# The mixer's output projection taken from rounded halves of z and of its weights, in three passes

## What is computed

```python
proj = jnp.einsum('bld,pd->blp', hidden_states, W_in)
gate = proj[..., :INTER]
...                                   # conv, chunked scan -> y  (B, L, INTER)
g = y * jax.nn.silu(gate)
gg = g.reshape(B, L, G, INTER // G)
var = jnp.mean(gg * gg, axis=-1, keepdims=True)
gg = gg * lax.rsqrt(var + EPS)
out_norm = gg.reshape(B, L, INTER) * norm_weight
return jnp.einsum('bli,di->bld', out_norm, W_out)
```

## Time and profile before

| what | before |
|---|---|
| median of 3 runs | 2531.27 us (2529.53 to 2531.35) |
| the profiled execution | 2531.68 us, span of the trace 2530.0 us |
| PE busy over the span | 2259.8 us, 89% |
| DVE, ACT, POOL busy | 1836.3 us (73%), 1435.5 us (57%), 1289.7 us (51%) |
| mixer's part (about 265 to 1518 us) | PE busy 1211.3 of 1253.0 us, granted clock 1.00 |
| output projection L981 | 256.4 us of PE, 1024 entries |

### The profile page before, as it was taken

The page is one execution under the profiler, slowest core; times in us unless marked ns, Lnnn a source line. Parts: engine busy times, 40 slices in busy tenths (PEclk is TensorE's granted clock), DMA queues, the critical chain, the costliest instruction groups (busy, mean ns, idle before and its releaser), DMA issues. The chain is left out here.

```text
span 2530.0 us, 45593 instructions
## 1 busy us (share of the span) xinstructions
PE 2259.8 (89%) x16164; PEld 1793.2 (71%) x16164; DVE 1836.3 (73%) x3256; ACT 1435.5 (57%) x2461; POOL 1289.7 (51%) x1275
## 2 busy tenths in 40 slices
PE   4996999999999999999999972799999995799992
PEld 2785788888888888888888862688888884444432
DVE  5875777777777777777777746677777776777755
ACT  1333778877878787877878851122222224266661
POOL 3451676777767777676876770354554540000000
PEclk9997999999999999999999995899999998799996
DMA  2002112112121121211211220100000002122214
GB/s 90 1 22 111 44 53 74 53 45 90 45 80 47 45 91 45 82 45 53 82 53 57 75 67 1 36 28 21 28 21 28 27 8 96 59 76 81 76 60 137
DMA packets 93441, 141.19 MB, mean 56 GB/s; under 512 B 23713, under 2 KB 62977, under 8 KB 91969
## 3 DMA queue, kind: packets, MB, share of 16 engines
q1 hardware_dynamic: 91200, 133.96, 16.1%
q10 hardware_dynamic: 2048, 4.72, 0.6%
HBM read 118.12 MB, written 20.32 MB: 55 GB/s over the span
## 5 line engine op out<-in xcount | busy, mean ns | idle before, releaser
L1081 DVE SCALAR_TENSOR_TENSOR mix_cv<-mix_pp,mix_cw,mix_cv 128x384 f32<-128x384 f32 (+4 forms) x864 | 490.8, 571 | 215.0 <-ACT mix_cv L999 194.2
L1220 POOL TENSOR_TENSOR ffn_hl<-ffn_h,ffn_hh 128x512 fp32r<-128x512 f32 x112 | 144.9, 1293 | 250.8 <-ACT ffn_hh L1278 250.8
L1024 ACT ACTIVATE mix_lm<-mix_pd 128x512 f32<-128x512 f32 x256 | 153.3, 599 | 205.1 <-PE mix_pd L915 203.1
L851 POOL TENSOR_TENSOR mix_ce<-mix_ce,mix_cv 128x1024 f32<-128x1024 f32 x112 | 266.8, 2382 | 0.0
L75 PE MATMUL mix_pp<-l0in_XH,mix_w_lo 128*128 128x384 f32 (+2 forms) x576 | 243.6, 423 | 22.9 <-DVE mix_w_lo L1069 16.2
L981 PE MATMUL mix_px<-mix_wo,mix_z 128*128 128x256 f32 x1024 | 256.4, 394 | 0.0
L1707 DVE TENSOR_REDUCE att_tops<-att_psc 128x1 f32<-128x512 f32 (+3 forms) x384 | 189.9, 550 | 55.5 <-PE att_psc L1655 32.2
L857 POOL TENSOR_TENSOR mix_zt<-mix_zsq 128x256 f32<-128x256 f32 x128 | 94.2, 736 | 243.0 <-ACT mix_zsq L1032 243.0
L1731 ACT ACTIVATE att_pr<-att_pst 128x1024 f32<-128x1024 f32 (+7 forms) x256 | 156.5, 657 | 103.5 <-PE att_pst L1672 73.5
L1278 ACT ACTIVATE ffn_hh<-ffn_h 128x512 fp32r<-128x512 f32 x112 | 71.1, 635 | 249.0 <-DVE ffn_h L1301 249.0
L981 PEld LDWEIGHTS mix_px<-mix_wo,mix_z 128*128 128x128 f32 x1024 | 186.8, 192 | 20.6
(11 more groups left out here) (332 smaller groups left out, 6873.2 us busy)
## 6 DMA issues: line engine op xcount, KB each, us to landing
mix_ce<-ecs SPq DMA_DIRECT2D x112, 512.0 KB, 3.7
mix_w_raw<-in_w_in SPq DMA_DIRECT2D x8, 1280.0 KB, 5.6
a_part<-att_sums SPq DMA_DIRECT2D x32, 256.0 KB, 5.1
ffn_raw<-in_wgu SPq DMA_DIRECT2D x56, 128.0 KB, 2.2
mix_ll<-cs SPq DMA_DIRECT2D x384, 4.0 KB
mix_wo<-in_w_out SPq DMA_DIRECT2D x8, 512.0 KB, 6.6
ffn_draw<-in_wd SPq DMA_DIRECT2D x28, 128.0 KB, 2.1
q<-qkv_part SPq DMA_DIRECT2D x24, 128.0 KB, 1.9
```

The source lines that it names most:

```text
L851: pool.tensor_tensor(ce[o][:, :, :], ce[o][:, :, :], cv[:, CT_C, cols_of(c)].unsqueeze(1).to_broadcast([P, GH, Q]), ALU.mult).then_inc(ce_ ...
L1024: act.activation(lm[o][:, 4 * i:4 * i + 4, :].rearrange("p h l -> p (h l)"), pd[:, :], ACT.Exp).then_inc(l_done, 1)
L1081: last = dve.scalar_tensor_tensor(out, of, cw[:, g, ct, 3 - d:4 - d], out, ALU.mult, ALU.add)
```

## The change

Rounded halves: `hi` is a value rounded to TensorE's fp32r format, `lo` the remainder in the same format. The product z times wo becomes zh·wo_l + zh·wo_h + zl·wo_h. The output weights are split once a group (`wo_h` by ScalarE, `wo_l` by GpSimd, in the slot `c % 16 == 1`), and z in every slot (`zh` by ScalarE behind the gate's SiLU, `zl` by GpSimd between `zs` and `xdt`). z and `wo` have one buffer now. The table constants that were loaded through the second z buffer go through `xtok0`.

```diff
-        wo = s.sb("wo", [P, 2, GX // P, D])
+        wo = s.sb("wo", [P, GX // P, D])
+        wo_h, wo_l = (s.sb(n, [P, GX // P, D], F32R) for n in ("wo_h", "wo_l"))
-        z = [s.sb(f"z{j}", [P, NX, Q]) for j in range(2)]
+        z = s.sb("z", [P, NX, Q])
+        zh, zl = (s.sb(n, [P, NX, Q], F32R) for n in ("zh", "zl"))
...
                     if c % 16 == 2 and g < G0 - 1:
                         wait(sp, proj_done, 36 * g)
                         wait(sp, gate_done, 16 * g)
-                        wait(sp, op_done, 16 * g)
+                        sp.wait_ge(wo_split, g + 1)
...
-                        pool.tensor_tensor(wo[:, o, :, :], wo[:, o, :, :],
+                        pool.tensor_tensor(wo[:, :, :], wo[:, :, :],
-                                           ALU.mult).then_inc(wo_split, 1)
+                                           ALU.mult).then_inc(wo_scaled, 1)
...
                         pool.tensor_tensor(zs[:, :], zt[:, 0, :], zt[:, 1, :], ALU.add).then_inc(zs_done, 1)
+                        if p % 16 == 0:
+                            pool.wait_ge(wo_cut, p // 16 + 1)
+                            pool.tensor_tensor(wo_l[:, :, :], wo[:, :, :], wo_h[:, :, :].bitcast(F32), ALU.subtract).then_inc(wo_split, 1)
+                        pool.wait_ge(zh_done, p + 1)
+                        wait(pool, op_done, p)
+                        pool.tensor_tensor(zl[:, :, :], z[:, :, :], zh[:, :, :].bitcast(F32), ALU.subtract).then_inc(zl_done, 1)
...
+                        pe.wait_ge(zh_done, p + 1)
                         for k in range(NX):
-                            last = pe.matmul(px[:, 0:D], z[p % 2][:, k, :], wo[:, p // 16 % 2, k, :],
-                                             start=k == 0, stop=k == NX - 1)
+                            pe.matmul(px[:, 0:D], zh[:, k, :], wo_l[:, k, :], start=k == 0, stop=False)
+                            pe.matmul(px[:, 0:D], zh[:, k, :], wo_h[:, k, :], start=False, stop=False)
+                        pe.wait_ge(zl_done, p + 1)
+                        for k in range(NX):
+                            last = pe.matmul(px[:, 0:D], zl[:, k, :], wo_h[:, k, :], start=False, stop=k == NX - 1)
                         last.then_inc(op_done, 1)
...
+                    if 0 <= p < NC:
+                        wait(act, op_done, p)
+                        if p % 16 == 0:
+                            act.wait_ge(wo_scaled, p // 16 + 1)
+                            act.activation(wo_h[:, :, :], wo[:, :, :], ACT.Copy).then_inc(wo_cut, 1)
+                        act.activation(flat(zh), flat(z), ACT.Copy).then_inc(zh_done, 1)
...
-                        wait(dve, op_done, p - 1)
-                        wait(dve, sq_done, p - 1)
-                        dve.tensor_tensor(z[p % 2][:, :, :], py[:, :].rearrange("p (k l) -> p k l", k=NX),
+                        wait(dve, sq_done, p)
+                        wait(dve, zh_done, p)
+                        wait(dve, zl_done, p)
+                        dve.tensor_tensor(z[:, :, :], py[:, :].rearrange("p (k l) -> p k l", k=NX),
```

More of the change, by code:

```diff
@@ L694, in mixer @@
         tabs_in, norm_in, const, made, self_v, zeroed = (s.sem(n) for n in ("tabs_in", "norm_in", "const", "made", "self_v", "zeroed"))
-        w_in_s, wx_split, wg_split, wo_split, hi_made, hi_first = (
-            s.sem(n) for n in ("w_in", "wx_split", "wg_split", "wo_split", "hi_made", "hi_first"))
+        w_in_s, wx_split, wg_split, wo_scaled, wo_cut, wo_split, hi_made, hi_first, zh_done, zl_done = (
+            s.sem(n) for n in ("w_in", "wx_split", "wg_split", "wo_scaled", "wo_cut", "wo_split", "hi_made", "hi_first", "zh_done",
+                               "zl_done"))
         cs_in, ecs_in = ([s.sem(f"{n}{j}") for j in range(2)] for n in ("cs_in", "ecs_in"))
@@ L707, in mixer @@
             s.sem(n) for n in ("xdt_done", "xdtd_done", "ce_done", "cd_done", "zt_done", "zs_done", "rs_done"))
-        rows_f, ones_f = z, zsq
+        ones_f = zsq
         def flat(ap):
@@ L770, in load_weights @@
                     sp.dma_start(w_raw[:, :, :], w_in[g]).then_inc(w_in_s, 16)
-                    sp.dma_start(wo[:, g % 2, :, :], w_out[g]).then_inc(w_in_s, 16)
+                    sp.dma_start(wo[:, :, :], w_out[g]).then_inc(w_in_s, 16)
                 def load_row(i):
@@ L783, in _ @@
                 for i in range(2):
-                    sp.dma_start(flat(rows_f[i])[0:KD_ROWS, :], sel_rows[:, i * 512:(i + 1) * 512]).then_inc(const, 16)
+                    sp.dma_start((flat(z) if i == 0 else xtok[0])[0:KD_ROWS, :], sel_rows[:, i * 512:(i + 1) * 512]).then_inc(const, 16)
                 sp.dma_start(flat(ones_f)[0:KD_ROWS, 0:2 * Q], one_rows).then_inc(const, 16)
@@ L1013, in _ @@
                         act.activation(rl[o][:, 4 * i:4 * i + 4, :].rearrange("p h l -> p (h l)"),
-                                       flat(rows_f[i])[0:KD_ROWS, :], ACT.Copy).then_inc(made, 1)
+                                       (flat(z) if i == 0 else xtok[0])[0:KD_ROWS, :], ACT.Copy).then_inc(made, 1)
                 act.wait_ge(tabs_in, 48)
@@ L1031, in _ @@
                         wait(act, zt_done, p)
-                        act.activation(flat(zsq), flat(z[p % 2]), ACT.Square).then_inc(sq_done, 1)
+                        act.activation(flat(zsq), flat(z), ACT.Square).then_inc(sq_done, 1)
                     if live:
```

## The result

| what | before | after |
|---|---|---|
| median of 4 runs | 2530.4 us (2527.1 to 2531.35) | 2643.53 us (2638.69 to 2646.95) |
| the profiled execution, its span | 2531.68, 2530.0 us | 2638.69, 2637.0 us |
| PE busy over the span | 2259.8 us, 89% | 2284.7 us, 87% |
| ACT, POOL busy | 1435.5, 1289.7 us | 1498.8, 1465.6 us |
| output projection on PE, by line | 256.4 us, 1024 entries (L981) | 138.2, 128.2 and 95.6 us, 1536 entries (L991, L992, L995) |

The change makes the kernel slower: 1.0449 of the time before, 95% interval 1.0436 to 1.0461. That is 113 us between the medians and 107.0 us between the two profiled spans.

A forecast was written before the change was run, and what follows sets the result against it. PE looked like the bound, with a four-engine loop through `xdt` 1.34 us of slack behind it. Terms 20 + 3 + 59.5 + 3.1 + 15 = 101 us on 2531.7 gave 2633 us, range 2576 to 2662.

The forecast's parts named there:

- PE's part: Output projection on PE: twelve matmuls take 1.5 us where the old ones took 1.81, saving 0.3 us a slot.
- Ordinary slots: 88 of 128 mixer slots: `zl` on POOL delays `xdt`, `py` waits for it, and each slot grows by 0.34 us.
- Slots with three fills: 32 of 128 slots, two of eight: PE's own work mostly covers the later `xdt`, so each gains 0.3 us.
- Weight pieces: Slots where POOL also makes a weight remainder piece: at most 0.8 us in four slots of seven groups; taken as +3.
- The start of a group: Slot `c % 16 == 1`: the `wo_l` chain costs 3.1 us; in seven groups late `ll` makes it 8.5 us.
- The clock: Behind each of the seven stalls for `ll`, PE runs at half clock: 2.2 us each, +15 us in all.
- Half clock in ordinary slots: Rival: PE's three waits per slot drop the clock once in eight slots, 26 us more, 2659; 7 in 100.
- PE alone sets the time: Rival, faster: the loop's slack holds, weights come early enough, only PE's saving of 38 us counts, 2493; 3 in 100.
- The weights are not late: Rival: at group starts SP's wait costs nothing beyond the chain, 48 us more in all, 2580; 8 in 100.

## Why the prediction was right, point by point

- **PE's part.** Twelve passes were put at 1.5 us for 1.81. In slot 63, where nothing holds them up, they take from 938.48 to 939.98, 1.50. PE's own saving was real, as the kernel with the remainder made once shows (1.49).
- **Ordinary slots: the step that was mis-sized.** The prediction put `py` at 872.46 instead of 872.12, 0.34 later. From `py` to `py` slot 62 grew by 0.40: 929.84 - 919.82 = 10.02, where before it was 872.12 - 862.50 = 9.62. The mechanism, POOL's `xdt` behind `zl`, was right, and its times too: `xdt` ends 929.70 - 919.82 = 9.88 behind the first `py`, as forecast (872.38 - 862.50 = 9.88). What was too small is the last step of the loop. The prediction let `py` start 0.08 behind `xdt`, the distance that it had read between ScalarE's square and GpSimd's `zt`; measured from `xdt` to `py` it is 0.14. So the slack was 1.42 - 0.14 = 1.28 us and not 1.34, and `xdt` came 1.68 later. Over 88 slots 0.06 is 5 us. The table's 30.0 for 80 slots, near the forecast's 30.2, does not show this: there 0.20 of an ordinary slot's cost goes to the slot behind it, and half clock adds 4.0. Two experiments show the mechanism from two sides: without `zl` the slot is 9.46 long, and with `xdt` ahead of `zl` the wait moves to the third pass and the slot grows to 10.40.
- **Slots with three fills.** The prediction let them gain 0.30, since the later `xdt` is "mostly covered by PE's own work". From `py` to `py` they gained 0.30. The -2.7 of the table is this gain less the 0.20 booked to them from the slot ahead.
- **Weight pieces.** +3 was forecast. From `py` to `py` the ordinary slots with a piece grew by 0.40 like those without, but for slot 5 of a group: 0.49 to 0.52 in each of seven groups, and 0.40 in the last one, which has no piece. That is 7 x 0.11 = 0.8 us, inside the bounds of 0 and 22.
- **The start of a group.** Forecast 3.1 for the chain and 8.5 for each stall; measured 3.7 and 8.7. `w_raw` left 10.01 us into the slot (9.8 forecast) and `ll` came 7.50 after it (7.3 forecast). That `wo`'s landing gives the time until the small tables behind it are there was the choice that held. Both experiments on SP's order confirm that the tables wait behind this load; what holds them there, the queue or the bytes ahead of them, is not shown.
- **The clock.** Forecast 2.2 us a stall; the slots behind a group start grew by 14.4 in all, 0.85 of it in the last group; (14.4 - 0.85 - 7 x 0.40) / 7 = 1.5 for each of the seven stalls. The reason is in the busy times above: of the 10.24 us at half clock only the 3.20 behind the stall count for the next slot, 1.6 of loss; the prediction had taken half of 4.40. The Trainium skill (TensorE: Matmul & The Clock Gate, section "What's actually happening") has the throttled state as the default that activity releases: the trace agrees, since the clock stays at half while PE waits, and for 3.20 us of work behind it.
- **Half clock in ordinary slots**, a rival with 7 in 100: it came, but at three places only (from 527.18, 868.52 and 1380.52), and cost 4.0 us instead of 26: slots 24 and 25, 56 and 57, 104 and 105 grew together by 1.97, 1.96 and 1.96, where the same slots of the other groups grew by some 0.62. The profiled run was the fastest of four. Its mean granted clock was 0.942; the others had 0.940, 0.940 and 0.937 and took 4.8, 4.9 and 8.3 us longer. By estimate 0.002 less over 2640 us is 10.6 us more at half clock, which costs up to 5.3, so more such stretches would account for the 6 us between the difference of the medians, 113, and that of the spans, 107. No trace of those runs shows them.
- **The other rivals.** "PE alone sets the time" would be right for the computation if the remainder had another place: that kernel took 2488, and the rival said 2493; that they are so near is in part chance, since waits of PE that the rival did not count fell and rose there too. "The weights are not late" is refuted by 49 and 69 us.
- **The sum.** The slots cost 106.4 us where their terms gave 100.9, and errors of both signs stand behind that: too low were ordinary slots (5), half clock among them (4) and the group starts (2), too high the clock behind the stalls (4) and the weight pieces (2). That the total came so near is in part luck; the terms above are what to trust.

## What to carry to other kernels

A saving on the bound engine is worth nothing if the instructions that feed it come later by as much: before adding a step to another engine's queue, ask what stands behind it there and how much slack that has (here 1.28 us against 1.68). A product that is taken apart into passes need not be done in one place: the passes that need the late operand can go where it is no longer late, and here that was worth more than the faster engine (90 us and 17). A wait for the buffer that a transfer fills also holds every transfer behind it in that queue (49 and 69 us here); move the small, urgent ones ahead of it.

## What the runs showed of the hardware that I had not expected

- The granted clock fell to half after a wait shorter than the 1.89 us that the trace of before had shown. PE at the end of slot 56 of the changed kernel, busy times behind it (slot 57 begins at 869.09), and PE at the end of slot 40, the same slot of the group before:

```profile
866.57 0.38 PE L983 MATMUL mix_pgt<-mix_one,mix_zs 128*128 128x1 f32 x2 [1.03 <-POOL mix_zs L863]
```
```profile
868.52:871.93 3.41, 3.41 (x25) 2.52 (x24) 1.93 (x4) 1.33 (x2) 3.41 (x4) 0.50 0.00 0
```
```profile
696.44 0.38 PE L983 MATMUL mix_pgt<-mix_one,mix_zs 128*128 128x1 f32 x2 [1.03 <-POOL mix_zs L863]
```

  The same wait of 1.03 us, but slot 57 has half clock behind it and is 10.13 us long, and slot 41 keeps the full clock and is 9.02 long. Five of the eight groups are like slot 41. What tells them apart the rows don't show.
- VectorE makes the same remainder in 721 ns that GpSimd makes in 1278 to 1293, and the weights' in 1216 instead of 2346: 1.8 and 1.9 times as fast. The Trainium skill (GPSIMD Engine Reference, section "4.1 Engine selection") gives GpSimd about half of VectorE's speed for elementwise operations with two inputs; the rows agree.
